# Third stage of a two-layer decoder kernel: attention probabilities transposed in pairs of 64-row tiles, eight heads at a time

## What is computed

```
x = x + L0_xattn(layernorm(x), ctx)     # 16 heads of 8 features, causal
x = x + L0_ffn(layernorm(x))            # 128 -> 512 -> 128
x = x + L1_xattn(layernorm(x), ctx)     # 16 heads of 64, relative positions, gate
x = x + L1_ffn(layernorm(x))            # 128 x 128, quantised to int8

# L1_xattn, per sequence and head n
attn = (hq @ hk.T + shifted(hq @ head_r.T) + biases) / sqrt(128)
attn = softmax(where(mask, -1e9, attn))       # 128 queries x 120 keys
out  = attn @ hv * sigmoid(q @ head_w)        # needs attn with keys first
out  = layernorm(out_all_heads @ Wo + residual) * ln_g + ln_b
```

## Time and profile before

| | |
|---|---|
| median of three runs | 478.32 us |
| the profiled execution | 480.16 us, span 478.4 us |
| PE busy | 449.8 us, 94% of the span |
| DVE busy | 398.6 us, 83% |
| ACT busy | 373.6 us, 78% |
| POOL busy | 256.2 us, 54% |
| granted TensorE clock, mean | 0.976 |
| third stage | about 184 us to 478 us |
| transposes L1158 of that stage | 256 matmuls, 38.8 us busy |

### The profile page before, as it was taken

How to read it: one execution, slowest core, us unless ns; L and a number is a source line. 1 busy time by engine, 2 the same in 40 slices (tenths; PEclk the granted TensorE clock), 3 DMA queues, 4 the chain that set the end, 5 groups by cost and what they waited for, 6 DMA issues and landing times.

```text
span 478.4 us, 15909 instructions
## 1 busy us (share of the span) xinstructions
PE 449.8 (94%) x5635; PEld 335.2 (70%) x5635; DVE 398.6 (83%) x1316; ACT 373.6 (78%) x1467; POOL 256.2 (54%) x370
## 2 busy tenths in 40 slices
PE   7988999999978998999999999999999999999981
PEld 6554556665655777768887887887888788788770
DVE  5798788988857895499779899899999989988974
ACT  1886679989874556579988888898898888888971
POOL 2566797787765662024245436535445544644694
PEclk9897899999999999999999999999999999999996
DMA  8041000000000000987465664654845656566200
GB/s 244 14 163 36 7 12 12 5 10 7 8 2 1 1 0 5 211 229 194 105 160 130 138 157 108 152 146 114 186 105 145 151 124 146 134 151 149 50 8 22
DMA packets 54383, 44.74 MB, mean 94 GB/s; under 512 B 43952, under 2 KB 49328, under 8 KB 54320
## 3 DMA queue, kind: packets, MB, share of 16 engines
q1 hardware_dynamic: 53328, 43.06, 37.1%
q10 hardware_dynamic: 992, 0.85, 0.5%
HBM read 22.92 MB, written 20.97 MB: 92 GB/s over the span
## 4 chain that ended last, share of the span: by engine, by line
PE 80%; ACT 6%; DVE 5%; POOL 2%; DMA 2%; issue 2%; SPq 2%; POOLq 0%; DVEq 0%; ACTq 0%
PE PS L982 66%; PE PS L1158 5%; PE PS L996 5%; ACT prob L491 2%; ACT prob L418 1%; PE PS L1140 1%; DMA wr<-in_wr 1%; DMA mask<-in_mask 1%; PE PS L1282 1%; POOL prob L302 1%; SPq L231 1%; PE PS L1130 1%; PE PS L1242 0%; DVE relw L731 0%; DVE relw L647 0%
## 5 line engine op out<-in xcount | busy, mean ns | idle before, releaser
L348 POOL TENSOR_TENSOR prob<-prob,rsum 128x480 f32<-128x480 f32 x64 | 63.2, 988 | 107.9 <-DVE rsum L864 58.1
L491 ACT ACTIVATE prob<-prob,nmax 128x120 f32<-128x120 f32 x256 | 98.6, 395 | 2.2 <-DVE nmax L956 2.2
L418 ACT ACTIVATE prob<-PS,nmax 128x120 f32<-128x120 f32 x256 | 88.8, 408 | 3.5 <-DVE nmax L654 3.4
L302 POOL TENSOR_TENSOR prob<-prob,rsum 128x480 f32<-128x480 f32 x64 | 62.4, 988 | 28.1 <-DVE rsum L703 14.5
L418 ACT ACTIVATION_READ_ACCUMULATOR prob<-PS,nmax 128x1 f32 x256 | 65.3, 255 | 0.0
L491 ACT ACTIVATION_READ_ACCUMULATOR prob<-prob,nmax 128x1 f32 x256 | 51.5, 201 | 0.0
L996 PEld LDWEIGHTS PS<-ident,prob 128*120 128x120 f32 x256 | 28.4, 140 | 30.4 <-POOL prob L302 12.6
L982 PE MATMUL PS<-rT,qv 64*32 64x152 f32 x2048 | 47.8, 295 | 1.4 <-DVE prob L837 0.8
L996 PE MATMUL PS<-ident,prob 128*120 128x128 f32 x256 | 38.1, 284 | 6.8 <-DVE v L663 3.1
L982 PE MATMUL PS<-xnT,wq 128*128 128x128 f32 x288 | 44.0, 289 | 0.4 <-ACT xnT L566 0.4
L982 PEld LDWEIGHTS PS<-ctx,wk 128*128 128x128 f32 x288 | 37.8, 195 | 7.7 <-issue 6.5
(11 more groups left out here) (195 smaller groups left out, 1111.1 us busy)
## 6 DMA issues: line engine op xcount, KB each, us to landing
rel_scratch<-relw SPq DMA_DIRECT2D x128, 152.0 KB, 2.7
relr<-rel_scratch SPq DMA_DIRECT2D x64, 240.0 KB, 4.1
ctx<-in_ctxT SPq DMA_DIRECT2D x32, 60.0 KB, 1.9
out_x<-fin SPq DMA_DIRECT2D x16, 64.0 KB, 1.6
x_all<-in_x SPq DMA_DIRECT2D x1, 640.0 KB, 6.8
wr<-in_wr SPq DMA_DIRECT2D x1, 512.0 KB, 5.2
wq<-in_wq SPq DMA_DIRECT2D x1, 512.0 KB, 4.0
wk<-in_wk SPq DMA_DIRECT2D x1, 512.0 KB, 4.8
```

What stands on the lines that cost most here:

```text
L302: return pool.tensor_tensor(pr, pr, cols(rsum[p], g, HG).unsqueeze(2).to_broadcast([S, HG, SK]), ALU.mult)
L348: return pool.tensor_tensor(pr, pr, cols(rsum[p], g, HG).unsqueeze(2).to_broadcast([S, HG, SK]), ALU.mult)
L418: last = act.activation(cols(prob[p], n, SK), cols(scores, q, SK), ACT.Exp, bias=nmax[p][:, n:n + 1], accum_out=ssum[p][:, n:n + 1])
L491: last = act.activation(cols(pr, n, SK), cols(pr, n, SK), ACT.Exp, bias=bias[:, n:n + 1], accum_out=total[:, n:n + 1])
```

## The change

Each head's 128 x 120 block is transposed as two matmuls, one for queries 0 to 63 (rows 0 to 63 of the array) and one for queries 64 to 127 (rows 64 to 127). Each has a 64 x 120 stationary operand and a 64 x 64 piece of the identity as the moving one. The first half of the queries goes to one PSUM bank, the second to another; eight heads of 64 columns fill each bank. T0 and T1 become one group of 16 matmuls at T1's old place (**T01**, banks 1 and 6), T2 and T3 one group at T3's old place (**T23**, banks 5 and 6). The semaphore `scaled` is split in four. ACT's four copies stay where they are in its order, but each now takes one query half of eight heads and writes it in 64-column pieces into a common `probT`; probT0 and probT1 both wait for T01, probT2 and probT3 both for T23. The products with `hv` wait for both copies. The core of the diff:

```diff
-        probT = ring("probT", [SK, HG * S])
+        probT_all = sb("probT", [SK, 2 * HG * S])
+        probT = [probT_all[:, 0:HG * S], probT_all[:, HG * S:2 * HG * S]]
...
# scalar engine; probT1, probT2 (2 * t + 2) and probT3 (2 * t + 2) likewise
-                    act.wait_ge(A1["probT_ps"], 4 * t + 1)
-                    act.activation(probT[0][:, :], PS[0:SK, 1, :], ACT.Copy).then_inc(A1["probT0"], 1)
+                    act.wait_ge(A1["probT_ps"], 2 * t + 1)
+                    act.activation(heads(probT_all, 2 * HG)[:, :, 0:DK], heads(PS[0:SK, 1, :], 2 * HG), ACT.Copy)\
+                        .then_inc(A1["probT0"], 1)
...
# tensor engine
-                def probs_transpose(p, g, bank):
-                    for q in range(HG):
-                        last = pe.transpose(PS[0:SK, bank, q * S:(q + 1) * S], cols(prob[p], g * HG + q, SK),
-                                            ident_sb[:, :])
+                def probs_transpose(p, g, banks):
+                    for q in range(2 * HG):
+                        for half, bank in enumerate(banks):
+                            rows = slice(half * DK, (half + 1) * DK)
+                            last = pe.transpose(PS[0:SK, bank, q * DK:(q + 1) * DK], cols(prob[p], g * HG + q, SK)[rows],
+                                                ident_sb[rows, rows])
                     return last
                 t, p = s - 4, par
                 if on(t):
+                    pe.wait_ge(A1["probT2"], t + 1)
                     pe.wait_ge(A1["probT3"], t + 1)
...
# T0's old place
-                    pe.wait_ge(A1["scaled"], 4 * t + 1)
-                    probs_transpose(p, 0, 1).then_inc(A1["probT_ps"], 1)
+                    pe.wait_ge(A1["scaled0"], t + 1)
+                    freed(pe, (A1["kT1"], t + 3, t + 2), (A1["probT3"], t, t - 1))
...
# T1's old place, after y_half
-                    pe.wait_ge(A1["scaled"], 4 * t + 2)
-                    freed(pe, (A1["kT1"], t + 3, t + 2), (A1["probT3"], t, t - 1))
-                    probs_transpose(p, 1, 6).then_inc(A1["probT_ps"], 1)
+                    pe.wait_ge(r_set, 4)
+                    pe.wait_ge(A1["scaled1"], t + 1)
+                    probs_transpose(p, 0, (1, 6)).then_inc(A1["probT_ps"], 1)
...
# before av1
+                    pe.wait_ge(A1["probT0"], t + 1)
                     pe.wait_ge(A1["probT1"], t + 1)
...
# T2's old place, after rel2
-                    pe.wait_ge(A1["scaled"], 4 * t + 3)
-                    probs_transpose(p, 2, 5).then_inc(A1["probT_ps"], 1)
...
# T3's old place, after acc
-                    pe.wait_ge(A1["scaled"], 4 * t + 4)
-                    probs_transpose(p, 3, 6).then_inc(A1["probT_ps"], 1)
+                    pe.wait_ge(r_set, 4)
+                    pe.wait_ge(A1["scaled2"], t + 1)
+                    pe.wait_ge(A1["scaled3"], t + 1)
+                    probs_transpose(p, 2, (5, 6)).then_inc(A1["probT_ps"], 1)
...
# before av2
                     freed(pe, (F1["deq"], t - 2, t - 3), (A1["ez"], t + 3, t + 2))
+                    pe.wait_ge(A1["probT2"], t + 1)
+                    pe.wait_ge(A1["probT3"], t + 1)
```

More of the change, by code:

```diff
@@ L177, in decoder_kernel @@
             "stats", "var", "stored0", "stored1", "relr00", "relr01", "relr10", "relr11", "relw3", "hv_ps",
-            "ctx_loaded0", "ctx_loaded1", "mask_loaded0", "mask_loaded1", "relw1", "rsum", "scaled", "xb", "ovar",
+            "ctx_loaded0", "ctx_loaded1", "mask_loaded0", "mask_loaded1", "relw1", "rsum", "scaled0", "scaled1", "scaled2", "scaled3", "xb", "ovar",
             "orstd", "rstd", "onorm", "og", "x_done", "av", "hv1", "probs", "nmax", "hq_ps", "qv1", "oT1",
@@ L352, in layer1 @@
                     pool.wait_ge(A1["rsum"], 4 * t + 3)
-                    scale_probs(p, 2).then_inc(A1["scaled"], 1)
+                    scale_probs(p, 2).then_inc(A1["scaled2"], 1)
                     pool.wait_ge(A1["rsum"], 4 * t + 4)
-                    scale_probs(p, 3).then_inc(A1["scaled"], 1)
+                    scale_probs(p, 3).then_inc(A1["scaled3"], 1)
                 t, p = s - 5, 1 - par
@@ L366, in layer1 @@
                     pool.wait_ge(A1["rsum"], 4 * t + 1)
-                    scale_probs(p, 0).then_inc(A1["scaled"], 1)
+                    scale_probs(p, 0).then_inc(A1["scaled0"], 1)
                 t, p = s - 4, par
@@ L378, in layer1 @@
                     pool.wait_ge(A1["rsum"], 4 * t + 2)
-                    scale_probs(p, 1).then_inc(A1["scaled"], 1)
+                    scale_probs(p, 1).then_inc(A1["scaled1"], 1)
                 t, p = s - 4, par
@@ L530, in layer1 @@
                 if on(t):
-                    act.wait_ge(A1["probT_ps"], 4 * t + 2)
-                    act.activation(probT[1][:, :], PS[0:SK, 6, :], ACT.Copy).then_inc(A1["probT1"], 1)
+                    act.wait_ge(A1["probT_ps"], 2 * t + 1)
+                    act.activation(heads(probT_all, 2 * HG)[:, :, DK:S], heads(PS[0:SK, 6, :], 2 * HG), ACT.Copy)\
+                        .then_inc(A1["probT1"], 1)
                 t, p = s - 2, par
@@ L578, in layer1 @@
                 if on(t):
-                    act.wait_ge(A1["probT_ps"], 4 * t + 3)
-                    act.activation(probT[0][:, :], PS[0:SK, 5, :], ACT.Copy).then_inc(A1["probT2"], 1)
+                    act.wait_ge(A1["probT_ps"], 2 * t + 2)
+                    act.activation(heads(probT_all, 2 * HG)[:, :, 0:DK], heads(PS[0:SK, 5, :], 2 * HG), ACT.Copy)\
+                        .then_inc(A1["probT2"], 1)
                 t, p = s - 6, par
@@ L594, in layer1 @@
                 if on(t):
-                    act.wait_ge(A1["probT_ps"], 4 * t + 4)
-                    act.activation(probT[1][:, :], PS[0:SK, 6, :], ACT.Copy).then_inc(A1["probT3"], 1)
+                    act.wait_ge(A1["probT_ps"], 2 * t + 2)
+                    act.activation(heads(probT_all, 2 * HG)[:, :, DK:S], heads(PS[0:SK, 6, :], 2 * HG), ACT.Copy)\
+                        .then_inc(A1["probT3"], 1)
                 t, p = s - 2, par
@@ L1309, in layer1 @@
                     last.then_inc(A1["rel_ps"], 1)
-                t, p = s - 3, 1 - par
-                if on(t):
-                    pe.wait_ge(A1["scaled"], 4 * t + 3)
-                    probs_transpose(p, 2, 5).then_inc(A1["probT_ps"], 1)
                 t, p = s + 1, 1 - par
```

## The result

The changed kernel takes **484.06 us** (median of four runs, 483.3 to 485.5), the kernel before, 478.53 (median of four). The ratio is 1.0126 with a 95% interval of 1.0089 to 1.0162: slower by 1.3%. All medians and extremes here are those of every execution, while the ratios are estimated from the fast executions alone and are not the quotients of these medians: three of the twelve executions of experiment 5 and one of the twelve of experiment 11 were slow, and without them their medians are 475.71 and 473.68. The forecast was 482.3, with a range of 476 to 487. Run once more (experiment 10), the change gave 484.53 and 1.0143 (1.0105 to 1.0181).

A forecast was written before the change was run, and what follows sets the result against it. PE's order bounds the kernel without slack; nine full steps at +0.36 (+3.2), steps 3 to 5 +0.3, step 15 -0.3 and the drain +0.8 sum to +4.0 on the median 478.32, giving 482.3 us, range 476 to 487.

The forecast's parts named there:

- The bound: PE is busy for all 17.22 us of a full step, so any change to its order shows in the time.
- The pair at 0.060: In T01 and T23, one pair of 64-row transposes costs 0.060 us, a group of 8 pairs 0.63.
- second rival: Pairs in T01 and T23 take 0.11 us each, 0.80 more per step, about 494 us; chance 0.12.
- Part 1: T0 and T1 become T01: y_half, T01 and hv take 2.56 us against 2.63, gain 0.07 per full step.
- Part 2: T2 and T3 become T23: T2's start to rel3's start falls from 1.97 to 1.77 us, gain 0.20.
- Part 3: hk waits for ACT's probT3, late because both copies wait for T23; PE stands 0.63 us per full step.
- first rival: ACT does not hold hk back, so PE's gain of 0.27 per step stands: 474.3 us; chance 0.14.
- Steps 4 and 5: No fin in these steps, so the stall is 0.36 us and each loses 0.09.
- Step 3: No fin in this step, so the stall is 0.36 us and it loses 0.09.
- Step 15: Last step with relative scores: no qv0, so hardly a stall, and 0.3 us gained.
- The drain: Steps 16 to 18: ACT passes on T23's 0.2 us delay, last av2 waits for probT3; +0.8 us.

The follow-up runs named there:

- experiment 5: Changed kernel with T23 moved right after rel2 and ACT's probT2 and probT3 together ahead of fin and qv0; 477.91 us, ratio 0.9967.
- experiment 11: experiment 5 for tiles 1 to 12; tiles 0 and 13 to 15 transposed whole, old places and ACT order; 473.98 us, ratio 0.9918.
- experiment 10: The changed kernel itself, unedited, timed once more against the kernel before; 484.53 us, ratio 1.0143.
- experiment 7: Changed kernel with all eight matmuls of one row half ahead of those of the other in each group; 493.7 us, ratio 1.0345.
- experiment 2: Changed kernel with T2 and T3 whole at their old places again, only T01 in pairs; 479.28 us, ratio 1.0017.
- Experiment 1: Changed kernel with ACT's order qv0, probT2, probT3, fin in place of probT2, fin, qv0, probT3; 476.84 us, ratio 0.9992.
- Experiment 8: Changed kernel with T23 and acc exchanged on PE, so T23 goes ahead of acc; 483.7 us, ratio 1.0129.
- Experiment 9: Changed kernel with the last three tiles (13 to 15) transposed whole at the four old places; 482.11 us, ratio 1.0114.
- experiment 6: experiment 5 with T01 at T0's old place ahead of y_half, that place's waits ahead of hk; 478.83 us, ratio 1.0026.

## Why the prediction was right, and where it was off

- **The bound** (PE's order, no slack): right. Steps follow PE's distances to 0.01 us wherever no wait is added.
- **The pair at 0.060**: right. From the first to the last of 16 matmuls pass 0.46 to 0.47 us, 0.11 for the first pair and 0.058 to 0.060 for each further one, and the load lasts 136 ns. The group costs 0.61 to 0.62, forecast 0.63. The second rival (0.11, 494 us) falls. The 493.7 us of experiment 7 come close to its number, and to its description too: halves that take turns. The change alternates, and there the halves overlap. The rule of the Trainium skill (TensorE: Matmul & The Clock Gate, "LDWEIGHTS (loading the stationary operand)"), columns over 1.2 whatever the rows, would give 0.10 per pair. The measured 0.059 speaks against it for transposing loads, and so does experiment 7, where matmuls on the same rows, each with a load of 120 columns, follow each other every 57 to 60 ns. The plain loads agree with the rule in the 0.09 to 0.10 by which they are exposed, not in their recorded 183 ns.
- **Part 1**: gain 0.07 forecast, 0.06 in the distances (2.57 against 2.63) and 0.05 in experiment 2. y2's wait on probT0 costs nothing in full steps, as costed.
- **Part 2**: gain 0.20 forecast, 1.97 - 1.76 = 0.21.
- **Part 3**, the stall at hk: 0.63 forecast, 0.62 by experiment 5 and the change. It comes in three pieces: rel3 to hv takes 0.08 more (hv's wait on probT2), which I called swallowed, hv to hk 0.46 more, and hk to av2 0.08 more (1.053 against 0.978). The sum is as forecast. The wait's entry shows 9 times 0.3 rather than 12 times 0.6, since hv's last matmul covers a part and in steps 3 to 5 the idle part is too short to be named. The first rival (474.3) falls: ACT does hold hk back. Experiment 1 shows that the reason is the order ACT works in.
- **Steps 4 and 5**: +0.09 each, as forecast. **Step 3**: forecast +0.09, measured +0.37, and the part that failed is T01. In that step no y_half stands between T0 and T1, and the copies are what av1 waits for. Before, probT0 could start after the first four transposes of eight, 3.63 into the step (219.38, from 215.75); now it waits for all sixteen and starts at 3.79 (217.20, from 213.41). probT1 stands two exponentials behind it, and av1 begins 5.72 into the step in place of 5.49:

```profile
217.20 0.60 ACT L526 ACTIVATE probT<-PS 120x512 f32<-120x512 f32 x1
218.45 0.58 ACT L534 ACTIVATE probT<-PS 120x512 f32<-120x512 f32 x1
219.13 0.66 PE L987 MATMUL PS<-probT,hv 120*64 120x128 f32 x8 [0.24 <-issue]
```

  The copy ends at 219.03 and av1 starts at 219.13, after 0.24 in which PE stands idle. The profile names no releaser there; that it is probT1 I read from the times. I had priced part 1 in the full step, where y2 and a bf16 transpose stand ahead of av1, and carried that over.
- **Step 15**: -0.3 forecast, -0.07 measured. T23 does not win its 0.20 there: this step has no hq, and rel3 comes so early that it stands for ACT's relw (PE's timeline):

```profile
433.73 0.75 PE L987 MATMUL PS<-rT,qv 64*32 64x152 f32 x32 [0.21 <-ACT relw L578]
```

- **The drain**: +0.8 forecast, +1.8 measured. This is the largest miss. For the last av2 I had 0.43 and 0.4, and the stretch from step 17 to the end lost 0.95, near that. For step 16 I let ACT pass on only the 0.2 by which T23 ends later than T2, and it lost 0.86. Missed was that T2 used to fill the time in which acc waits for ez: without it acc waits 0.36, and T23 stands behind acc. Experiment 8 gives 0.58 of this back. Experiment 9 gives back nearly all of the 1.8. How the 0.95 divides between the form of the transposes and av2's new wait on probT3 no run parts.

So the sum was +4.0 and is +5.5: +0.3 step 3, +0.2 step 15, +1.0 the drain. The odds leaned the wrong way for the same reason: within 1% of before had 0.61, and slower by over 1%, which came, 0.34. Mechanism, place and sign were right; the three misses lie in the steps where the pipeline is partly filled, and in each an instruction is absent whose cover I had counted on.

What stays open: why step 2 takes 12.3 to 13.1 us, from execution to execution, whichever kernel it is; why the timed median of experiment 6 does not show the 2.0 us by which its profiled stage is shorter; and the division of the drain's last 0.95.

## What to carry to other kernels

When several results are gathered into one group, price the consumers as well as the group: PE won 0.27 us per step here and gave back 0.62, because two copies that had been spread out now became ready together, and the last of them stood behind work on ACT that had nothing to do with it. Move the gathered group to the earliest place of its members and put its copies side by side in the consumer's order; either alone brought only a part (17.08 to 17.18, and 17.03, against 16.95 with both). Where the pipeline fills and drains, cost the edit again, since the instructions that hid a wait in the full step may not be there.

## What was not expected of the hardware

- Row halves of the array need alternation in the queue: the same sixteen matmuls take 0.61 to 0.62 us alternating and 0.90 to 0.92 one half after the other (each half has its own bank, see experiment 7).
- The clock fell in the middle of the drain in some executions. With T01 alone, av2 waited 1.73 us (before 454.45), and the eight output projections after it took 1.85 us from start to start, against 1.09 at full clock in the changed kernel (460.22 to 461.31). Busy time by stretch (the clock is the third number from the end; 0.66 is a mean of time at 2.4 and at 1.2 GHz), T01 alone:

```profile
455.00:460.00 5.00, 5.00 (x46) 4.32 (x43) 1.93 (x11) 3.19 (x13) 4.68 (x10) 0.66 0.04 13
```

  In the changed kernel a gap of 1.70 stands at the same place without such a fall, and in experiment 7 the clock fell after gaps of 0.30, 0.36 and 0.69 only, so the length of one stand does not decide it; what does, these runs do not show. The fall also touched experiments 7 and 8, so their way from step 17 to the end (35.07 and 32.98) is not compared here. At the very end the lower level is there in every trace: in the last 9.4 us of before the mean is 0.50, with four small bf16 matmuls left.
- The first stages vary by themselves. The 30 us from 30 to 60 were at a mean clock of 0.83 in the profiled execution of before and of 0.94 in that of after, in code that the change does not touch, and the third stage began 2.35 us sooner. Single spans therefore don't tell a change of 1%; distances within full steps do.
